# Adding the causal mask of the first attention on VectorE instead of TensorE

## The chip, the core and the metric

The program runs on one core of a Trainium2 chip. Five engines work side by side, each through its own queue in strict order: PE (TensorE, matmuls; its weight loads are listed as PEld), DVE (VectorE), ACT (ScalarE), POOL (GpSimd) and SP (SyncE, which issues DMAs here). They wait for each other through semaphores. The metric is the device time of one execution in microseconds (us); lower is better.

## The reference

Two transformer layers over 2 sequences of 1024 tokens and 256 channels. Only the first attention is touched by the change:

```python
q = einsum('bsd,hed->bhse', x, W_Q)          # 16 heads of width 128, k and v alike
scores = einsum('bhse,bhme->bhsm', q, k) / sqrt(128)
scores = where(causal, -1e9, scores)         # causal: key index > query index
pattern = softmax(scores)
z = einsum('bhsm,bhme->bhse', pattern, v)
out = einsum('bhse,hde->bsd', z, W_O)
```

After it come a layer norm, a mixture of 8 experts with a shared one, a second attention with grouped keys, and a mixture of 16 experts.

## The kernel before

Every matmul of fp32 data is done three times, with operands split into a high part (rounded to fp32r by ACT) and a low part (the difference, taken by DVE or POOL): `mm3` (L80 to L88) issues high x high at L86, and two cross terms at L87 and L88.

The first attention is `causal_attention`. It takes 32 "heads", numbered `hb` (16 heads of two sequences), one after the other. A head has 8 units, `qt` 0 to 7, one for each tile of 128 queries; tile `qt` has `(qt + 1) * 128` keys, so the keys beyond the diagonal block are never computed and only the diagonal 128x128 block needs a mask. A unit's scores lie in PSUM in one of two buffers, `s_ps[:, qt % 2]`.

What one tile goes through, with the engine of each step:

- PE `scores`: the three matmuls for every 512 keys, then one matmul of identity and mask that adds the mask to the diagonal block (L876) and reports `s_ready`.
- DVE `maximum` (L1054): negated row maximum `negm`, reports `max_done`.
- ACT `soften` (L972): exp of the scores with their sum, into `pr`, reports `exp_done`.
- DVE `invert` (L1063): reciprocal of the sum. POOL `normalise` (L830): `pr` times that, reports `p_done`.
- PE `turn` (L886): transposes of `pr` into `t_ps`, in one batch of up to 4 blocks or in two.
- ACT `keep_hi` (L979) writes `pth`; DVE `keep_lo` (L1070) writes `ptl` and frees the `t_ps` buffer (`tl_done`), of which there are two.

The steps of several tiles run at once. In unit `qt`, the order written out by hand is:

- PE: `scores(qt + 2)`, `turn(qt)`, then the unit's tasks
- ACT: `keep_hi(qt)`, `soften(qt + 2)`, then the tasks' high parts
- DVE: `invert(qt + 1)`, `maximum(qt + 2)`, `keep_lo(qt)`, then the tasks' low parts

Here `qt + 2` beyond 7 means a tile of the next head. Below, a prime marks such a tile: in unit 6 DVE takes the maximum of tile 0'. The tasks are the projections of the next head (`q`, `k`: high part at L1003, low part at L1088 and L1091), the product with the values (`pv`, for queries 512 to 1023 of the last head in unit 0, and for 0 to 511 in unit 4; it gives `zh`, `zl`), and the output projection `o` (added into `yT` by DVE, L1082). Each fourth head (`hb % 4 == 0`, called a lead head here) has one more task in each unit, the values of four heads (`v`). The other 24 are called plain heads. Three of these (17 to 19) carry the norm and the router of the first sequence too. All tasks share two PSUM banks, so a task on PE waits until DVE has emptied that of the last but one.

Of the kernel before, what the change touches and what calls it, by code (L numbers as in the profile page):

```python
# [8 lines left out]
F32R = mybir.dt.float32r  # L9
ACT = mybir.ActivationFunctionType  # L10
ALU = mybir.AluOpType
AX = mybir.AxisListType

P = 128
# [68 lines left out]
def mm3(pe, out, a_hi, a_lo, b_hi, b_lo, first, last):  # L83


    pe.matmul(out, a_hi, b_hi, start=first, stop=False)  # L86
    pe.matmul(out, a_hi, b_lo, start=False, stop=False)  # L87
    return pe.matmul(out, a_lo, b_hi, start=False, stop=last)  # L88
# [524 lines left out]
def causal_attention(nc, tag, counters, a, xh, xl, yT, ident, idr, eps, psum, rw, norm, router):  # L613
# [5 lines left out]
    NQ = S // P  # L619
# [5 lines left out]
    MASKED = -1.0e30  # L625
# [44 lines left out]
    with Phase(nc, tag, psum) as ph:  # L670
# [10 lines left out]
        qh = ph.sb("qh", [P, 2, S], F32R)  # L681
        ql = ph.sb("ql", [P, 2, S], F32R)
        kh = ph.sb("kh", [P, 2, S], F32R)
        kl = ph.sb("kl", [P, 2, S], F32R)
# [7 lines left out]
        negm = ph.sb("negm", [P, NP])  # L692
        rsum = ph.sb("rsum", [P, NP])
        rinv = ph.sb("rinv", [P, NP])
        mask0 = ph.sb("mask0", [P, P])
        mask = ph.sb("mask", [P, P], F32R)
        s_ps = ph.ps([P, 2, S])
        t_ps = ph.ps([P, 2, CH])
        r_ps = ph.ps([P, 2, CH])
# [1 line left out]
        cleared = ph.sem("cleared")  # L701
# [3 lines left out]
        mask_set = ph.sem("mask_set")  # L705
        rounded = ph.sem("rounded")
# [8 lines left out]
        wol_done = ph.sem("wol_done")  # L715
        s_ready = ph.sem("s_ready")
        max_done = ph.sem("max_done")
        exp_done = ph.sem("exp_done")
        inv_done = ph.sem("inv_done")
        p_done = ph.sem("p_done")  # L720
# [42 lines left out]
        def after(hb, qt):  # L763

            u = hb * NQ + qt
            return u // NQ, u % NQ

        @block.sync
        def _(sp):
            def load_x(c):  # L770
                t = slice(c * CH, (c + 1) * CH)
                sp.dma_start(yT[:, :, t], a["xT"][:, :, t]).then_inc(y_in[c], 16)

            def load(n):
                if n >= 2:

                    sp.wait_ge(wl_done, (n - 1) * 2)
                sp.dma_start(wr[:, n % 2], a["qkv0"][n % H0, :, 0:2]).then_inc(wr_in[n % 2], 16)

            def load_v(g):  # L780
                if g >= 1:
                    sp.wait_ge(wvl_done, g)
                h0 = g * VG % H0
                for h in range(VG):
                    sp.dma_start(wvr[:, :, h, :], a["qkv0"][h0 + h, :, 2]).then_inc(wv_in, 16)

            def load_o(n):
                if n >= 1:
                    sp.wait_ge(wol_done, n)
                sp.dma_start(wor[:], a["o0"][n % H0]).then_inc(wor_in, 16)  # L790

            load(0)
            load_x(0)
            load_x(1)
            load_v(0)
            load(1)
            load_o(0)
            load_x(2)
            load_x(3)
            rw.sync(sp)  # L800
            for hb in range(HB):
                if hb + 2 < HB:
                    load(hb + 2)
                if hb + 1 < HB:
                    load_o(hb + 1)
                if hb % VG == 0 and hb + VG < HB:
                    load_v(hb // VG + 1)

        @block.gpsimd
        def _(pool):  # L810
            def split(n):
                pool.wait_ge(wh_done, n + 1)
                for w in range(2):
                    pool.tensor_tensor(wl[:, n % 2, w].rearrange("p t e -> p (t e)"), wr[:, n % 2, w].rearrange("p t e -> p (t e)"),
                                       wh[:, n % 2, w].rearrange("p t e -> p (t e)").bitcast(F32),
                                       ALU.subtract).then_inc(wl_done, 1)

            def split_v(g):
                pool.wait_ge(wvh_done, g + 1)
                pool.tensor_tensor(wvl[:].rearrange("p t e -> p (t e)"), wvr[:].rearrange("p t h e -> p (t h e)"),  # L820
                                   wvh[:].rearrange("p t e -> p (t e)").bitcast(F32), ALU.subtract).then_inc(wvl_done, 1)

            def split_o(n):
                pool.wait_ge(woh_done, n + 1)
                pool.tensor_tensor(wol[:], wor[:], woh[:].bitcast(F32), ALU.subtract).then_inc(wol_done, 1)

            def normalise(hb, qt):
                pool.wait_ge(inv_done, hb * NQ + qt + 1)
                j, n = qt % NP, (qt + 1) * P
                pool.tensor_tensor(pr[j][:, 0:n], pr[j][:, 0:n], rinv[:, j:j + 1].to_broadcast([P, n]),  # L830
                                   ALU.mult).then_inc(p_done, 1)

            pool.memset(ident[:], 0.0).then_inc(cleared, 1)
            pool.memset(mask0[:], 0.0).then_inc(cleared, 1)
            pool.memset(eps[:], EPS).then_inc(eps_set, 1)
            pool.wait_ge(cleared, 1)
            pool.affine_select(out=ident[:], in_=ident[:], compare_op=ALU.not_equal, fill=1.0, base=0,
                               pattern=[[-1, P]], channel_multiplier=1).then_inc(ident_done, 1)
            pool.wait_ge(cleared, 2)

            pool.affine_select(out=mask0[:], in_=mask0[:], compare_op=ALU.is_ge, fill=MASKED, base=0,
                               pattern=[[-1, P]], channel_multiplier=1).then_inc(mask_set, 1)
            split(0)
            split_v(0)
            normalise(0, 0)
            split(1)
            split_o(0)
            for hb in range(HB):
                for qt in range(NQ):
                    if after(hb, qt + 1)[0] < HB:  # L850
                        normalise(*after(hb, qt + 1))
                    if qt == 2 and hb + 2 < HB:
                        split(hb + 2)
                    if qt == 4 and hb >= 1:
                        split_o(hb)
                    if qt == 5 and hb % VG == 2 and hb + 2 < HB:
                        split_v(hb // VG + 1)

        @block.tensor
        def _(pe):  # L860
            def scores(hb, qt):
                u = hb * NQ + qt
                if qt == 0:
                    pe.wait_ge(task_out, PLACE[hb - 1, ("k", 0)] + 1)
                if qt == CQ:
                    pe.wait_ge(task_out, PLACE[hb - 1, ("k", 1)] + 1)
                if u >= 2:

                    pe.wait_ge(exp_done, u - 1)
                q0, s = qt * P, hb % 2  # L870
                keys = q0 + P
                for k0 in range(0, keys, CH):
                    k1 = min(keys, k0 + CH)
                    mm3(pe, s_ps[:, qt % 2, k0:k1], qh[:, s, q0:q0 + P], ql[:, s, q0:q0 + P], kh[:, s, k0:k1], kl[:, s, k0:k1],
                        True, k1 < keys)
                pe.matmul(s_ps[:, qt % 2, q0:q0 + P], idr[:], mask[:], start=False, stop=True).then_inc(s_ready, 1)  # L876

            def turn(hb, qt):
                pe.wait_ge(p_done, hb * NQ + qt + 1)
# [59 lines left out]
            pe.wait_ge(ident_done, 1)  # L939
            for t in PRE:  # L940
                task((-1, t))
            pe.wait_ge(rounded, 2)
            for qt in range(2):
                scores(0, qt)
            for hb in range(HB):
                for qt, tasks in enumerate(PLANS[hb]):
                    if qt < NQ:
                        if after(hb, qt + 2)[0] < HB:
                            scores(*after(hb, qt + 2))
                        turn(hb, qt)  # L950
                    for t in tasks:
                        if t[0] == "side":
                            t[1].tensor(pe, t[2], ring)
                        else:
                            task((hb, t))

        @block.scalar
        def _(act):
# [51 lines left out]
                task((-1, t))  # L1010
            act.wait_ge(mask_set, 1)
            act.wait_ge(eps_set, 1)
            act.activation(mask[:], mask0[:], ACT.Copy).then_inc(rounded, 1)
            act.activation(idr[:], ident[:], ACT.Copy).then_inc(rounded, 1)
            for t in PRE[2:]:
                task((-1, t))
# [28 lines left out]
        def _(dve):  # L1045
# [5 lines left out]
            def maximum(hb, qt):  # L1051
                dve.wait_ge(s_ready, hb * NQ + qt + 1)
                n = (qt + 1) * P
                dve.tensor_reduce(negm[:, qt % NP:qt % NP + 1], s_ps[:, qt % 2, 0:n], AX.X, ALU.max,  # L1054
                                  negate=True).then_inc(max_done, 1)

# [40 lines left out]
            for qt in range(2):  # L1097
                maximum(0, qt)
# [656 lines left out]
def program(nc, a, out):  # L1755
    with ExitStack() as stack:
# [51 lines left out]
        with Phase(nc, "g") as g:  # L1808
            rw0 = RouterWeights(g, "rw0", w0, True)
            n0a = norm(g, "n0a", 0)  # L1810
            r0a = router(g, "r0a", 0, rw0, "n0a")
            causal_attention(nc, "a0", counters, a, xh, xl, yT, ident, idr, eps, psum, rw0, n0a, r0a)

            z = [g.sb(f"z{b}", [P, S // P, D]) for b in range(B)]
# [136 lines left out]
```

## Time and profile before

| | us |
|---|---|
| median of 3 runs | 2251.52 |
| lowest and highest of them | 2243.45, 2257.3 |
| the profiled execution, device time | 2240.75 |
| its span, first to last instruction | 2238.6 |
| mean granted TensorE clock | 0.977 |

Of the 2238.6 us, the first attention takes about the first 990; its heads are periodic, four by four. The profiled execution is 10.8 us (0.5%) below the median of the three runs. 2.15 us of its time lie outside the span. Matmul durations in the trace run from issue to the last result, so they overlap: what a matmul costs PE is read from the distance between the starts of neighbours, not from its own duration.

### The profile page before, as it was taken

How to read it: one execution, taken by the hardware profiler on the slowest of the kernel's cores; microseconds unless marked ns; L12 is line 12 of the kernel's file. 1: busy time of each engine (PE TensorE's matmuls, PEld its weight loads, DVE VectorE, ACT ScalarE, POOL GpSimd, SP SyncE). 2: the span in 40 equal slices, each digit the busy share in tenths (PEclk: the TensorE clock that was granted, in tenths of full speed). 3: DMA queues.
4: the chain of work that ended last, by engine and by line, in shares of the span. 5: the costliest groups of instructions: out<-in, count | busy, mean ns of one | idle time of the engine just before them, and what ended most of it. 6: DMA issues, size and time to landing. Idle time of an engine off the chain costs nothing. (4 is left out here: it accounts for less than half of the span.)

```text
span 2238.6 us, 30499 instructions
## 1 busy us (share of the span) xinstructions
PE 2125.4 (95%) x11008; PEld 1608.0 (72%) x11008; DVE 1455.6 (65%) x2505; ACT 1207.5 (54%) x2425; POOL 556.9 (25%) x543
## 2 busy tenths in 40 slices
PE   7999999999999999989999968999998699999998
PEld 5888888888888888867788853333333487787886
DVE  4666666666766666656656547888883656645554
ACT  5655556565656565534444442877777334434344
POOL 3433434343424343322222210000000012221221
PEclk9999999999999999999999995999999799999999
DMA  2000000000000000011111120100000011111111
GB/s 80 15 9 24 15 24 15 24 15 24 8 24 15 24 15 15 6 31 46 43 43 43 43 42 16 23 16 22 16 22 1 27 36 43 43 50 43 48 45 61
DMA packets 54297, 64.74 MB, mean 29 GB/s; under 512 B 9179, under 2 KB 34566, under 8 KB 54150
## 3 DMA queue, kind: packets, MB, share of 16 engines
q1 hardware_dynamic: 54150, 62.81, 10.1%
q8 instruction: 89, 1.46, 0.3%
q14 instruction: 58, 0.48, 0.1%
HBM read 52.68 MB, written 2.10 MB: 24 GB/s over the span
## 5 line engine op out<-in xcount | busy, mean ns | idle before, releaser
L830 POOL TENSOR_TENSOR a_pr<-a_pr,a_rinv 128x128 f32<-128x128 f32 (+7 forms) x256 | 294.2, 1149 | 514.9 <-DVE a_rinv L1063 514.7
L1675 DVE TENSOR_REDUCE a_negm<-psum 128x1 f32<-128x1024 f32 x256 | 301.4, 1219 | 49.2 <-PE psum L1553 48.4
L1227 POOL TENSOR_TENSOR f_lo_gu<-f_raw_gu,f_hi_gu 128x512 fp32r<-128x512 f32 x84 | 108.9, 1296 | 848.4 <-ACT f_hi_gu L1313 848.4
L1656 ACT ACTIVATE a_pt<-psum 128x512 f32<-128x512 f32 x512 | 268.2, 602 | 81.8 <-PE psum L1568 81.5
L86 PE MATMUL psum<-xh,f_hi_gu 128*128 128x512 f32 x672 | 269.4, 401 | 7.0 <-DVE f_hid L1385 6.8
L1396 DVE TENSOR_TENSOR f_hl<-f_hid,f_hh 128x512 fp32r<-128x512 f32 x168 | 116.6, 694 | 236.6 <-ACT f_hh L1338 234.8
L88 PE MATMUL psum<-xh,f_lo_gu 128*128 128x512 f32 x672 | 263.8, 393 | 0.0
L87 PE MATMUL psum<-xl,f_hi_gu 128*128 128x512 f32 x672 | 263.5, 392 | 0.0
L1327 ACT ACTIVATE f_act_s<-psum,f_bias 128x512 f32<-128x512 f32 x168 | 115.1, 685 | 270.6 <-PE psum L88 270.4
L979 ACT ACTIVATE a_pth<-psum 128x512 fp32r<-128x512 f32 (+3 forms) x384 | 174.7, 490 | 142.9 <-PE psum L886 140.5
L972 ACT ACTIVATE a_pr<-psum,a_negm 128x128 f32<-128x128 f32 (+7 forms) x256 | 190.4, 744 | 81.8 <-DVE a_negm L1054 76.9
L1553 PE MATMUL psum<-x_ks,a_qq 48*128 48x512 f32 x512 | 186.3, 475 | 19.3 <-DMA a_qq<-x_qlo 14.5
L1070 DVE TENSOR_TENSOR a_ptl<-psum,a_pth 128x512 fp32r<-128x512 f32 (+3 forms) x384 | 200.3, 549 | 6.1 <-ACT a_pth L979 5.7
L1054 DVE TENSOR_REDUCE a_negm<-psum 128x1 f32<-128x128 f32 (+7 forms) x256 | 189.5, 741 | 2.9 <-PE psum L876 0.7
L1338 ACT ACTIVATE f_hh<-f_hid 128x512 fp32r<-128x512 f32 x168 | 105.5, 628 | 158.9 <-DVE f_hid L1390 151.8
L886 PE MATMUL psum<-ident,a_pr 128*128 128x128 f32 x1152 | 171.8, 276 | 10.7 <-POOL a_pr L830 9.0
L1568 PE MATMUL psum<-a_qq,x_ks 49*128 49x512 f32 x512 | 171.2, 480 | 4.5 <-ACT a_pt L1656 4.1
L1568 PEld LDWEIGHTS psum<-a_qq,x_ks 49*128 49x128 f32 x512 | 67.8, 187 | 138.5 <-ACT a_pt L1656 136.6
L86 PEld LDWEIGHTS psum<-xh,f_hi_gu 128*128 128x128 f32 x672 | 127.3, 189 | 40.2 <-DVE f_hid L1385 10.2
L1385 DVE SCALAR_TENSOR_TENSOR f_hid<-psum,f_bias,f_act_s 128x512 f32<-128x512 f32 x168 | 125.2, 745 | 43.8 <-PE psum L88 33.5
L1091 DVE TENSOR_TENSOR a_zl<-psum,a_zh 128x512 fp32r<-128x512 f32 x64 | 44.2, 691 | 161.5 <-ACT a_zh L1003 161.5
L1553 PEld LDWEIGHTS psum<-x_ks,a_qq 48*128 48x128 f32 x512 | 95.8, 200 | 74.4 <-DVE a_negm L1675 44.5
(299 smaller groups left out, 4823.4 us busy)
## 6 DMA issues: line engine op xcount, KB each, us to landing
f_raw_gu<-in_gu SPq DMA_DIRECT2D x84, 256.0 KB, 2.7
f_raw_dn<-in_down SPq DMA_DIRECT2D x84, 128.0 KB, 2.0
a_wr<-in_qkv SPq DMA_DIRECT2D x32, 256.0 KB, 2.8
a_wvr<-in_qkv SPq DMA_DIRECT2D x32, 128.0 KB, 2.5
a_wor<-in_o SPq DMA_DIRECT2D x32, 128.0 KB, 2.0
a_qq<-x_qhi SPq DMA_DIRECT2D x128, 32.0 KB, 2.0
yT<-in_xT SPq DMA_DIRECT2D x4, 512.0 KB, 6.2
a_qq<-x_qlo SPq DMA_DIRECT2D x64, 32.0 KB, 2.0
```

Of the source, the lines that this page charges most:

```text
L86: pe.matmul(out, a_hi, b_hi, start=first, stop=False)
L87: pe.matmul(out, a_hi, b_lo, start=False, stop=False)
L88: return pe.matmul(out, a_lo, b_hi, start=False, stop=last)
L830: pool.tensor_tensor(pr[j][:, 0:n], pr[j][:, 0:n], rinv[:, j:j + 1].to_broadcast([P, n]), ALU.mult).then_inc(p_done, 1)
L972: act.activation(pr[qt % NP][:, 0:n], s_ps[:, qt % 2, 0:n], ACT.Exp, bias=negm[:, qt % NP:qt % NP + 1], accum_out=rsum[:, qt % NP:qt % NP ...
L979: act.activation(pth[c][:, rows_of(c, k0, count, qt % CQ), :], t_ps[:, n % 2, 0:count * P].rearrange("p (k q) -> p k q", q=P), ACT.Copy).t ...
L1054: dve.tensor_reduce(negm[:, qt % NP:qt % NP + 1], s_ps[:, qt % 2, 0:n], AX.X, ALU.max, negate=True).then_inc(max_done, 1)
L1070: dve.tensor_tensor(ptl[c][:, p, :], t_ps[:, n % 2, 0:count * P].rearrange("p (k q) -> p k q", q=P), pth[c][:, p, :].bitcast(F32), ALU.sub ...
L1553: m = pe.matmul(mx_ps[:, bank, half, :], qq[p0:p0 + ROWS, u % QSLOT, g % 2, q * P:(q + 1) * P], ks[b][p0:p0 + ROWS, g % 2, half * CH:(half ...
L1568: pe.matmul(st_ps[:, n % 3, :], ks[b][p0:p0 + ROWS + 1, g % 2, kt * P:(kt + 1) * P], qq[p0:p0 + ROWS + 1, u % QSLOT, g % 2, :], start=True ...
L1656: act.activation(pt[:, s % SLOTS, g, :], st_ps[:, n % 3, :], ACT.Exp, scale=1.0 / HD1).then_inc(exp_done, 1)
L1675: dve.tensor_reduce(negm[:, u % 2, g * NQ + q:g * NQ + q + 1], mx_ps[:, bank, :, :], AX.XY, ALU.max, negate=True).then_inc(mx_taken, 1)
```

## The change

PE no longer adds the mask. The last of the three score matmuls closes the sum and reports `s_ready`. DVE, at the head of `maximum`, adds the mask, now an fp32 tile that POOL makes once, to the diagonal block in place in PSUM, waits for that add to be finished (`masked`) and then takes the maximum. ACT no longer rounds the mask once to fp32r.

```diff
             pool.memset(ident[:], 0.0).then_inc(cleared, 1)
-            pool.memset(mask0[:], 0.0).then_inc(cleared, 1)
+            pool.memset(mask[:], 0.0).then_inc(cleared, 1)
...
                 for k0 in range(0, keys, CH):
                     k1 = min(keys, k0 + CH)
-                    mm3(pe, s_ps[:, qt % 2, k0:k1], qh[:, s, q0:q0 + P], ql[:, s, q0:q0 + P], kh[:, s, k0:k1], kl[:, s, k0:k1],
-                        True, k1 < keys)
-                pe.matmul(s_ps[:, qt % 2, q0:q0 + P], idr[:], mask[:], start=False, stop=True).then_inc(s_ready, 1)
+                    i = mm3(pe, s_ps[:, qt % 2, k0:k1], qh[:, s, q0:q0 + P], ql[:, s, q0:q0 + P], kh[:, s, k0:k1],
+                            kl[:, s, k0:k1], True, True)
+                i.then_inc(s_ready, 1)
...
-            pe.wait_ge(rounded, 2)
+            pe.wait_ge(rounded, 1)
...
-            act.activation(mask[:], mask0[:], ACT.Copy).then_inc(rounded, 1)
             act.activation(idr[:], ident[:], ACT.Copy).then_inc(rounded, 1)
...
             def maximum(hb, qt):
                 dve.wait_ge(s_ready, hb * NQ + qt + 1)
                 n = (qt + 1) * P
+                own = s_ps[:, qt % 2, n - P:n]
+                if (hb, qt) == (0, 0):
+                    dve.wait_ge(mask_set, 1)
+                dve.tensor_tensor(own, own, mask[:], ALU.add).then_inc(masked, 1)
+                dve.wait_ge(masked, hb * NQ + qt + 1)
                 dve.tensor_reduce(negm[:, qt % NP:qt % NP + 1], s_ps[:, qt % 2, 0:n], AX.X, ALU.max,
                                   negate=True).then_inc(max_done, 1)
```

On DVE, units 1 to 3 of head 1, a plain head. Before (a_zl belongs to the end of unit 0; a_ql is the low part of the `q` task of unit 1):

```order
54 L1091 TENSOR_TENSOR a_zl<-psum,a_zh 128x512 [waits side_rounded]
55 L1063 RECIPROCAL a_rinv<-a_rsum 128x1 [waits a0_p_done,a0_exp_done]
56 L1054 TENSOR_REDUCE a_negm<-psum 128x1 [waits a0_s_ready]
57 L1070 TENSOR_TENSOR a_ptl<-psum,a_pth 128x2x128 [waits a0_th_done]
58 L1088 SCALAR_TENSOR_TENSOR a_ql<-psum,a_qh 128x512 [waits side_rounded]
59 L1063 RECIPROCAL a_rinv<-a_rsum 128x1 [waits a0_p_done,a0_exp_done]
60 L1054 TENSOR_REDUCE a_negm<-psum 128x1 [waits a0_s_ready]
```

and in the changed kernel:

```order
66 L1095 TENSOR_TENSOR a_zl<-psum,a_zh 128x512 [waits side_rounded]
67 L1067 RECIPROCAL a_rinv<-a_rsum 128x1 [waits a0_p_done,a0_exp_done]
68 L1056 TENSOR_TENSOR psum<-psum,a_mask 128x128 [waits a0_s_ready]
69 L1058 TENSOR_REDUCE a_negm<-psum 128x1 [waits a0_masked]
70 L1074 TENSOR_TENSOR a_ptl<-psum,a_pth 128x2x128 [waits a0_th_done]
71 L1092 SCALAR_TENSOR_TENSOR a_ql<-psum,a_qh 128x512 [waits side_rounded]
72 L1067 RECIPROCAL a_rinv<-a_rsum 128x1 [waits a0_p_done,a0_exp_done]
73 L1056 TENSOR_TENSOR psum<-psum,a_mask 128x128 [waits a0_s_ready]
74 L1058 TENSOR_REDUCE a_negm<-psum 128x1 [waits a0_masked]
```

One add stands ahead of every maximum, in all 256 units; the maximum waits for it, and all else keeps its order.

On PE, the border of units 0 and 1 of the same head: the scores of tile 3, the transposes of tile 1, and the `q` task. Before:

```order
356 L86 MATMUL psum<-a_kh,a_qh 128x512 [waits a0_exp_done]
357 L87 MATMUL psum<-a_kl,a_qh 128x512
358 L88 MATMUL psum<-a_kh,a_ql 128x512
359 L876 MATMUL psum<-a_mask,idr 128x128
360 L886 MATMUL psum<-ident,a_pr 128x128 [waits a0_tl_done,a0_p_done]
361 L886 MATMUL psum<-ident,a_pr 128x128
362 L86 MATMUL psum<-xh,a_wh 128x512 [waits a0_wl_done,side_emptied]
```

and in the changed kernel:

```order
337 L86 MATMUL psum<-a_kh,a_qh 128x512 [waits a0_exp_done]
338 L87 MATMUL psum<-a_kl,a_qh 128x512
339 L88 MATMUL psum<-a_kh,a_ql 128x512
340 L886 MATMUL psum<-ident,a_pr 128x128 [waits a0_tl_done,a0_p_done]
341 L886 MATMUL psum<-ident,a_pr 128x128
342 L86 MATMUL psum<-xh,a_wh 128x512 [waits a0_wl_done,side_emptied]
```

The matmul of L876 is gone, and the transposes follow the scores at once; PE's waits are the same.

## Rows read from the trace of the kernel before

**Rows 1.** The page, part 1: busy time, share of span, instructions.

```profile
PE 2125.4 (95%) x11008; PEld 1608.0 (72%) x11008; DVE 1455.6 (65%) x2505; ACT 1207.5 (54%) x2425; POOL 556.9 (25%) x543
```

**Rows 2.** One window inside the first attention: busy us by engine, clock.

```profile
784.00:896.00 112.00, 110.56 (x625) 96.10 (x625) 74.20 (x152) 66.81 (x146) 46.66 (x44) 1.00 0.05 15
```

**Rows 3.** Groups by line, 60 to 1150 us: busy, mean ns, idle before and releaser.

```profile
L972 ACT ACTIVATE a_pr<-psum,a_negm 128x384 f32<-128x384 f32 (+1 forms) x246 | 183.6, 746 | 76.3 <-DVE a_negm L1054 71.4
L1054 DVE TENSOR_REDUCE a_negm<-psum 128x1 f32<-128x384 f32 (+1 forms) x246 | 183.0, 744 | 2.7 <-PE psum L876 0.4
L876 PE MATMUL psum<-a_mask,idr 128*128 128x128 f32 x246 | 58.2, 236 | 0.0
```

**Rows 4.** Timeline (start, us, engine), PE at the mask matmul, units 5 and 6.

```profile
435.06 0.39 PE L88 MATMUL psum<-a_kh,a_ql 128*128 128x512 f32 x1
...
435.29 0.22 PE L876 MATMUL psum<-a_mask,idr 128*128 128x128 f32 x1
...
435.35 0.82 PE L886 MATMUL psum<-ident,a_pr 128*128 128x128 f32 x6
...
437.68 0.27 PE L876 MATMUL psum<-a_mask,idr 128*128 128x128 f32 x1
437.79 0.95 PE L886 MATMUL psum<-ident,a_pr 128*128 128x128 f32 x7
```

**Rows 5.** Groups by line and shape on DVE, 60 to 970 us.

```profile
L1070 DVE TENSOR_TENSOR a_ptl<-psum,a_pth 128x256 fp32r<-128x256 f32 x61 | 25.2, 413 | 0.0
L1070 DVE TENSOR_TENSOR a_ptl<-psum,a_pth 128x128 fp32r<-128x128 f32 x62 | 17.4, 280 | 0.0
```

**Rows 6.** Timeline of DVE: an operation that waits for the one before it.

```profile
2228.94 0.41 DVE L226 BATCH_NORM_STATS2 g_n3b_stats<-psum 128x6 f32<-128x256 f32 x1
2229.39 0.25 DVE L229 BATCH_NORM_AGGREGATE g_n3b_mv<-g_n3b_stats 128x2 f32<-128x6 f32 x2
```

**Rows 7.** Timeline, head 13, units 1 to 3: DVE and ACT in turn.

```profile
422.83 0.69 DVE L1091 TENSOR_TENSOR a_zl<-psum,a_zh 128x512 fp32r<-128x512 f32 x1 [4.95 <-ACT a_zh L1003]
...
423.51 0.67 DVE L1054 TENSOR_REDUCE a_negm<-psum 128x1 f32<-128x512 f32 x1
...
424.21 0.69 ACT L972 ACTIVATE a_pr<-psum,a_negm 128x512 f32<-128x512 f32 x1 [0.60 <-DVE a_negm L1054]
...
425.51 0.69 DVE L1088 SCALAR_TENSOR_TENSOR a_ql<-psum,a_qh 128x512 fp32r<-128x512 f32 x1 [1.00 <-ACT a_qh L1003]
...
426.12 0.15 DVE L1063 RECIPROCAL a_rinv<-a_rsum 128x1 f32<-128x1 f32 x1
```

**Rows 8.** Timeline, head 13, units 3 to 6: where ACT or DVE wait for PE.

```profile
430.39 0.60 ACT L1003 ACTIVATE a_kh<-psum 128x512 fp32r<-128x512 f32 x1 [0.38 <-PE psum L88]
...
434.07 0.60 ACT L1003 ACTIVATE a_zh<-psum 128x512 fp32r<-128x512 f32 x1 [0.17 <-PE psum L88]
...
435.31 0.15 DVE L1063 RECIPROCAL a_rinv<-a_rsum 128x1 f32<-128x1 f32 x1
...
435.55 1.23 DVE L1054 TENSOR_REDUCE a_negm<-psum 128x1 f32<-128x1024 f32 x1
...
440.16 0.60 ACT L1003 ACTIVATE a_kh<-psum 128x512 fp32r<-128x512 f32 x1 [0.17 <-PE psum L88]
```

**Rows 9.** Timeline, head 13, unit 7 and the next head's first transpose.

```profile
439.38 1.90 POOL L830 TENSOR_TENSOR a_pr<-a_pr,a_rinv 128x1024 f32<-128x1024 f32 x1 [1.95 <-DVE a_rinv L1063]
...
441.33 1.09 PE L886 MATMUL psum<-ident,a_pr 128*128 128x128 f32 x8
...
442.65 1.29 DVE L1070 TENSOR_TENSOR a_ptl<-psum,a_pth 128x512 fp32r<-128x512 f32 x2
...
443.56 0.27 PE L886 MATMUL psum<-ident,a_pr 128*128 128x128 f32 x1
```

**Rows 10.** Timeline, head 14, unit 7: DVE's wait in such heads.

```profile
469.33 1.29 DVE L1070 TENSOR_TENSOR a_ptl<-psum,a_pth 128x512 fp32r<-128x512 f32 x2 [0.35 <-ACT a_pth L979]
```

**Rows 11.** Timeline, lead head 12, unit 6: DVE's wait there.

```profile
410.02 0.69 DVE L1091 TENSOR_TENSOR a_kl<-psum,a_kh 128x512 fp32r<-128x512 f32 x1 [0.57 <-ACT a_kh L1003]
```

More of the change, by code:

```diff
@@ L694, in causal_attention @@
         rinv = ph.sb("rinv", [P, NP])
-        mask0 = ph.sb("mask0", [P, P])
-        mask = ph.sb("mask", [P, P], F32R)
+        mask = ph.sb("mask", [P, P])
         s_ps = ph.ps([P, 2, S])
@@ L717, in causal_attention @@
         max_done = ph.sem("max_done")
+        masked = ph.sem("masked")
         exp_done = ph.sem("exp_done")
@@ L839, in _ @@
             pool.wait_ge(cleared, 2)
-            pool.affine_select(out=mask0[:], in_=mask0[:], compare_op=ALU.is_ge, fill=MASKED, base=0,
+            pool.affine_select(out=mask[:], in_=mask[:], compare_op=ALU.is_ge, fill=MASKED, base=0,
                                pattern=[[-1, P]], channel_multiplier=1).then_inc(mask_set, 1)
```

## The prediction

> **What bounds the kernel now.** Start with the page's part 1: PE is busy 95% of the span, DVE 65% [rows 1]. In a window inside the first attention PE is busy 110.56 of 112 us at a granted clock of 1.00, DVE 74.20, ACT 66.81, POOL 46.66 [rows 2]. Read alone, that says that anything taken from PE is gained and that DVE has room for more. Two further views correct it. The groups by line show who waits for whom: ACT's exp sat idle 71.4 us for DVE's maximum, while DVE's maximum hardly ever waited for PE (0.4 us) [rows 3]. So DVE is not ahead of the scores but behind them, and ACT hangs on DVE. The timeline of one plain head then shows that DVE and ACT hand work to each other with hardly a gap: the maximum of tile 3 ends at 424.18, exp starts at 424.21; the high part of `q` follows that exp on ACT, its low part starts on DVE at 425.51, and the next reciprocal follows [rows 7]. PE is full, but a chain over DVE and ACT is nearly as long as PE's own, and it is reset only in unit 0, where the long `pv` leaves DVE idle 4.95 us [rows 7]. At the end of a plain head the chain already holds PE up: the transposes of tile 7 start at 441.33, when POOL's 1.90 us from 439.38 are over at 441.28 [rows 9].
>
> **What is removed.** 256 mask matmuls. Their mean duration is 236 ns [rows 3], but durations overlap. At the end of a 512-column score matmul the starts are 435.06, 435.29 and 435.35: the mask holds PE for 0.06 us [rows 4]. Where the last score matmul has 128 columns, the mask starts at 437.68 and the transposes at 437.79: 0.11 us [rows 4]. Tiles 0 and 4 of a head are of the second kind, the other six of the first (also with 256 or 384 columns in the last part), so a head saves 6 x 0.06 + 2 x 0.11 = 0.58 us where PE sets the pace, and all 32 at most 18.6 us. ACT's one rounding of the mask and the wait for it are gone too, once, for nothing that I can count.
>
> The Trainium skill, "TensorE: Matmul & The Clock Gate", section "Back-to-back issue gap", gives about 81 ns for each 128-column load and matmul in a stream; by that the 256 would be worth 20.7 us, an estimate. The trace's 0.06 and 0.11 lie on either side of it.
>
> **What is added.** 256 adds of 128x128 on DVE, PSUM and SBUF in, PSUM out, and a wait of DVE for its own result. No DVE row of this trace writes PSUM. The nearest is the low part of 128x128, PSUM and SBUF in, SBUF out: 280 ns [rows 5]. An operation that waits for its predecessor starts after its end: 2229.35 to 2229.39, 0.04 us [rows 6]. One that does not wait starts some 0.08 us before that end: `a_ql` ends at 426.20 (425.51 + 0.69), the reciprocal starts at 426.12 [rows 7]. So one add delays its maximum by p = 0.28 + 0.04 = 0.32 us. The low end for p is 0.20 (280 ns less the overlap of 0.08, a wait that costs nothing); the high end is 0.45, that of an operation twice as wide, 413 ns [rows 5], and 0.04. I take 0.32, since the 280 ns row differs only in where it writes. The one wait for `mask_set` in tile 0 of head 0 is over long before.
>
> Behind the waiting maximum on DVE are queued the low parts of the transposes and of the tasks; behind the late maximum on ACT are exp, then the high part of a task, for which DVE waits again. So one late maximum delays both engines. With 8 adds a head this is 2.6 us of work in a chain that has less slack than that. Follow it through head 13.
>
> **The walk, plain head.** The chain starts fresh after `pv` of unit 0. Seven maxima lie on it until DVE has freed the transpose buffer that PE needs for the first transpose of the next head (tiles 3, 4, 5, 6, 7, 0', 1'): 7 p. Slack on the way takes something back. Before `a_kh` of unit 3, ACT waits 0.38 us for PE; before `a_zh` of unit 4, 0.17; the maximum of tile 7 starts at 435.55 although the reciprocal ahead of it lets it go at 435.38, since the scores came late, 0.17; before `a_kh` of unit 6 ACT waits 0.17 [rows 8]. Last, of the low parts in unit 7 (442.65 on, 1.29 us for two, so the first ends near 443.34) PE's transpose at 443.56 needs the first, and needs it 0.05 earlier (POOL's end at 441.28 to PE's start at 441.33 shows this latency): 0.17 [rows 9]. The slack is 0.38 + 4 x 0.17 = 1.06 us. A plain head gets 7 x 0.32 - 1.06 = 1.18 us longer. PE's saving is then worth nothing in it: PE arrives earlier and waits longer, in the transposes of tiles 3, 6 and 7 and of tile 0'.
>
> In the plain heads with `hb % 4 == 2` POOL has the next weights of `v` to split before it normalises tile 7, and DVE waits 0.35 us for ACT in unit 7 [rows 10]; that much more is absorbed: 0.83 us. Six regular heads are of this kind (after head 26 no weights are left to prepare).
>
> **Lead head.** The `v` task gives PE work in each unit that DVE and ACT need less for. In unit 6 DVE waits 0.57 us before `a_kl` [rows 11], more than the 0.32 that the add puts ahead of it. Here PE's saving is real, 0.58 us.
>
> **The sum.** Regular plain heads: 15 x 1.18 = 17.7. Those with POOL's split: 6 x 0.83 = 5.0. The three that host norm and router have more on PE, and I give them half, 3 x 0.6 = 1.8. Lead heads: 8 x -0.58 = -4.6. Together +19.9 us; on the profiled execution's 2240.75 that is 2260.7, or +0.89%. The runs shown have a median 0.5% above that execution; applied to the median, 2251.5 x 1.0089 = 2271.5. A measurement of this kernel can tell about 1%, 22.5 us, from no change. The sum depends on p by 7 x 21 + 10 = 157 us for each us (seven adds in 21 heads, and half of that in the three hosts): p = 0.20 gives +1.1, p = 0.45 gives +40.3.
>
> **Rivals.**
> First, PE alone counts: all delay on DVE and ACT fits in slack that I don't see. Then 32 x 0.58 = 18.6 us are gained, 2233. For it: PE's 95%. Against: the walk, and the transposes of tile 7 that wait for POOL already.
> Second, the wait on DVE costs nothing, p between 0.20 and 0.28: +1.1 to +13.6, 2253 at the low end. Against: the gap of 0.04 after an end against an overlap of 0.08 [rows 6, 7]. The Trainium skill states this rule in "VectorE: DVE Perf Modes", section "The DRAIN you can't avoid": 8 copies with a semaphore after each took as long as 8 with one after the last. By that rule 2253 would come out; the trace does not agree with it, since operations without a wait overlap there.
> Third, slower: the add in place costs more than the row of 280 ns, because it writes its 128 columns to PSUM, where it also reads, and the maximum must find them there. Its place is the same chain, its price 157 us for each us, and it decides from p = 0.337 on, where the sum passes 22.5 us. At p = 0.45 it is 2251.5 + 40.5 = 2292. For it: only 0.017 us separate it from my value, and no row prices the write. Against: nothing in rows 5 hints at it.
> That the change does not do what it says is excluded: 256 matmuls are gone from PE and as many adds stand on DVE.
>
> **How the numbers follow.** My forecast (p from 0.28 to 0.337, walk as above) gets 0.43, the first rival 0.07, the second 0.12, the third 0.38. Only the first rival at its best reaches 1% faster: 0.02. Slower by over 1% is the third: 0.38. The rest, 0.60, is within 1%. The range runs from 2240, between the first rival and the low p, to the third rival's 2292.
>
> **What would show each step.** L876 gone from PE; DVE busy up by 256 x 0.28 = 72 us. Add rows of about 280 ns, the maximum some 0.32 us after the add's start. ACT's idle before exp for DVE up from 71.4 us. PE's waits for POOL's `a_pr` and DVE's `a_ptl` up; a plain head's period up by about 1.2 us, a lead head's down by 0.6. I am wrong if the add is not near 0.28 us, if ACT or DVE keep more slack than the five places hold, or if the clock, 1.00 in the window [rows 2], falls because PE waits more.

## The result, and the profile after

| | before | changed |
|---|---|---|
| median of 4 runs, us | 2250.76 | 2276.92 |
| lowest, highest | 2243.45, 2257.3 | 2267.94, 2277.83 |
| profiled execution, span | 2240.75, 2238.6 | 2277.32, 2275.2 |

The changed kernel takes 1.0108 times as long, 95% interval 1.0068 to 1.0148: 24 us more (the two medians in the table lie 26 us apart). The forecast was 20 us more. The value lies slightly above the 1% that the prediction took as the least that can be told from no change, but the interval reaches to both sides of 1%, so which side of it the true value lies on isn't settled.

The page of the changed kernel, part 1, answers to [rows 1]:

```profile
PE 2137.4 (94%) x10752; PEld 1586.4 (70%) x10752; DVE 1524.2 (67%) x2761; ACT 1199.4 (53%) x2424; POOL 556.7 (24%) x543
```

256 instructions fewer on PE, 256 more on DVE, whose busy time is up by 68.6 us. The groups by line, from 60 to 1150 us as in [rows 3], with the new add:

```profile
L1058 DVE TENSOR_REDUCE a_negm<-psum 128x1 f32<-128x384 f32 (+1 forms) x246 | 187.2, 761 | 8.5
L972 ACT ACTIVATE a_pr<-psum,a_negm 128x384 f32<-128x384 f32 (+1 forms) x246 | 183.3, 745 | 182.3 <-DVE a_negm L1058 182.3
...
L1056 DVE TENSOR_TENSOR psum<-psum,a_mask 128x128 f32<-128x128 f32 x246 | 69.0, 280 | 0.0
```

The add takes 280 ns, exactly what the row of the same shape that writes to SBUF took [rows 5]. ACT's idle time before exp rose from 71.4 to 182.3 us. What waits for that is seen in the waits of PEld from 60 to 1000 us (total, times, longest). Before:

```profile
PEld psum L886 <- POOL a_pr L830: 13.2, 25, 1.9
PEld psum L86 <- DVE yT L1082: 2.5, 7, 0.4
```

Changed:

```profile
PEld psum L886 <- POOL a_pr L830: 39.2, 69, 2.5
...
PEld psum L86 <- DVE yT L1086: 5.9, 9, 0.7
```

PE waits for POOL's `a_pr` in 69 transposes instead of 25. The same can be followed in the timeline of the changed kernel, head 13, units 1 to 3, against [rows 7]:

```profile
430.71 0.69 DVE L1095 TENSOR_TENSOR a_zl<-psum,a_zh 128x512 fp32r<-128x512 f32 x1 [4.61 <-ACT a_zh L1003]
...
431.39 0.28 DVE L1056 TENSOR_TENSOR psum<-psum,a_mask 128x128 f32<-128x128 f32 x1
...
431.70 0.69 DVE L1058 TENSOR_REDUCE a_negm<-psum 128x1 f32<-128x512 f32 x1
...
432.43 0.69 ACT L972 ACTIVATE a_pr<-psum,a_negm 128x512 f32<-128x512 f32 x1 [1.00 <-DVE a_negm L1058]
...
434.33 0.15 DVE L1067 RECIPROCAL a_rinv<-a_rsum 128x1 f32<-128x1 f32 x1
434.40 0.28 DVE L1056 TENSOR_TENSOR psum<-psum,a_mask 128x128 f32<-128x128 f32 x1
...
434.72 0.82 DVE L1058 TENSOR_REDUCE a_negm<-psum 128x1 f32<-128x640 f32 x1
...
435.66 0.66 PE L886 MATMUL psum<-ident,a_pr 128*128 128x128 f32 x4 [0.21 <-POOL a_pr L830]
```

Each maximum starts 0.31 to 0.32 us after its add, and the delay travels: the reciprocal after `a_ql` comes 3.62 us after `a_zl` began (434.33 - 430.71), before it was 3.29 (426.12 - 422.83, [rows 7]); the transposes of tile 3, which had not waited, now wait for POOL. At the head's end, against [rows 9]:

```profile
449.92 1.09 PE L886 MATMUL psum<-ident,a_pr 128*128 128x128 f32 x8 [0.41 <-POOL a_pr L830]
...
451.55 1.28 DVE L1074 TENSOR_TENSOR a_ptl<-psum,a_pth 128x512 fp32r<-128x512 f32 x2
...
452.38 0.30 PE L886 MATMUL psum<-ident,a_pr 128*128 128x128 f32 x1
```

The start of the first transpose of each head (the row of 452.38 is that of head 14) gives the length of a head. Before, heads 12, 13, 14 and 15 start at 378.00, 416.22, 443.56 and 470.22; in the changed kernel at 386.02, 424.04, 452.38 and 479.71. The lead head 12 went from 38.22 to 38.02 us, the plain head 13 from 27.34 to 28.34, head 14 (POOL's split) from 26.66 to 27.33. The three hosts together, from the start of head 17 to that of 20, went from 91.23 (534.75 to 625.98) to 96.48 (545.00 to 641.48), and head 0 from 38.67 to 39.38. With these as samples of their kinds, 15 x 1.00 + 6 x 0.67 + 5.25 - 7 x 0.20 + 0.71 = 23.6 us. The last transpose of the first attention starts at 976.3 before and at 1000.1 after, 23.8 us later.

The two profiled executions differ by 36.6 us, 12.8 more than that. These 12.8 us lie behind the first attention, in code that the change doesn't touch. Windows counted from the last transpose show where, in the clock column (the last but two). Before:

```profile
976.00:1300.00 324.00, 313.90 (x1400) 252.61 (x1398) 195.57 (x323) 138.28 (x246) 71.91 (x70) 0.98 0.17 46
1300.00:1400.00 100.00, 73.21 (x270) 39.60 (x268) 65.00 (x85) 34.54 (x63) 3.59 (x4) 0.71 0.11 23
1700.00:1800.00 100.00, 77.68 (x375) 44.31 (x375) 38.44 (x101) 45.62 (x83) 5.32 (x5) 0.88 0.07 20
```

Changed:

```profile
1000.00:1324.00 324.00, 313.84 (x1399) 252.43 (x1398) 195.81 (x323) 138.58 (x247) 71.83 (x70) 0.98 0.16 46
1324.00:1424.00 100.00, 73.70 (x250) 39.14 (x248) 62.41 (x82) 31.70 (x57) 3.59 (x4) 0.66 0.12 23
1724.00:1824.00 100.00, 78.53 (x339) 39.27 (x336) 33.54 (x95) 45.25 (x83) 3.29 (x3) 0.76 0.05 15
```

The granted clock is a mean over its two levels, 1.2 and 2.4 GHz. The second window of each three lies at the start of the second attention, the third at its end; PE is busy 73 to 79 of 100 us there in either kernel. In both, the clock was lower in this execution (0.66 for 0.71, 0.76 for 0.88). That this belongs to the execution and not to the change is shown below.

### The profile page after: what moved, and what is told of

It is laid out like the page before. It is cut to its first block and busy times, and to the rows that moved or that the text cites. A ratio compares the mean times of both kernels' runs of the same rounds, so it can differ in the third digit from the quotient of the medians.

```text
span 2275.2 us, 30243 instructions
## 1 busy us (share of the span) xinstructions
PE 2137.4 (94%) x10752; PEld 1586.4 (70%) x10752; DVE 1524.2 (67%) x2761; ACT 1199.4 (53%) x2424; POOL 556.7 (24%) x543
## 5 line engine op out<-in xcount | busy, mean ns | idle before, releaser
L1572 PE MATMUL psum<-a_qq,x_ks 49*128 49x512 f32 x512 | 176.2, 494 | 4.2 <-ACT a_pt L1660 3.7
L886 PEld LDWEIGHTS psum<-ident,a_pr 128*128 128x128 f32 x1152 | 132.7, 141 | 58.7 <-POOL a_pr L830 40.7
```

The lines of the kernel that those rows point to most:

```text
L886: i = pe.transpose(t_ps[:, n % 2, k * P:(k + 1) * P], pr[qt % NP][:, (k0 + k) * P:(k0 + k + 1) * P], ident[:])
L1572: pe.matmul(st_ps[:, n % 3, :], ks[b][p0:p0 + ROWS + 1, g % 2, kt * P:(kt + 1) * P], qq[p0:p0 + ROWS + 1, u % QSLOT, g % 2, :], start=True ...
```

## The experiments

The table has the length of heads 12 (lead), 13 (plain) and 14 (plain, with POOL's split), from the starts of their first transposes, the start of the attention's last transpose, the span behind it, and the time against the kernel before with its interval. Each ratio is against runs of the kernel before made together with those of that kernel. Two columns need care. The span behind the last transpose differs by up to 18 us between traces of the same code, as shown at the end. The last transpose also holds the start-up and head 0, whose length follows the granted clock there: head 1 begins at 58.6 in the second trace of before (clock 0.96 in head 0), at 60.6 in the first (0.92) and at 62.9 in e9_lead_not5 (0.85). So differences of up to 4 us in that column are judged from the heads instead.

| kernel | 12 | 13 | 14 | last transpose | behind it | ratio |
|---|---|---|---|---|---|---|
| before | 38.22 | 27.34 | 26.66 | 976.3 | 1262.3 | 1 |
| changed | 38.02 | 28.34 | 27.33 | 1000.1 | 1275.1 | 1.0108 (1.0068 to 1.0148) |
| e1_no_mask | 37.65 | 27.04 | 26.42 | 965.9 | 1265.8 | 0.9933 (0.9911 to 0.9955) |
| e2_add_only | 38.59 | 28.27 | 27.32 | 1003.9 | 1264.1 | 1.0118 (1.0075 to 1.0162) |
| e3_add_early | 38.02 | 28.41 | 27.37 | 1001.4 | 1264.7 | 1.0111 (1.0069 to 1.0153) |
| e4_lead_only | 38.04 | 27.32 | 26.68 | 973.8 | 1277.4 | 1.0018 (0.9995 to 1.0041) |
| e5_placed | 37.65 | 27.11 | 26.59 | 973.1 | 1275.2 | 0.9991 (0.9970 to 1.0012) |
| e8_late_tiles | 38.24 | 27.85 | 26.90 | 987.0 | 1277.4 | 1.0068 (1.0038 to 1.0099) |
| e9_lead_not5 | 37.71 | 27.34 | 26.66 | 974.8 | 1268.0 | one run |
| e7_two_adds | 39.18 | 30.82 | 29.63 | 1066.0 | 1264.9 | 1.0423 (1.0390 to 1.0455) |
| e10_placed_hosts | 37.69 | 27.16 | 26.54 | 968.4 | 1280.1 | 0.9965 (0.9943 to 0.9986) |
| e11_before_again | 38.19 | 27.31 | 26.66 | 974.2 | 1262.1 | one run |

The theory on trial is that of the walk: in plain heads a chain over DVE and ACT sets the length, the adds lengthen it by 0.32 us each less some slack, and PE's saving counts in lead heads only. Its rival: PE sets the pace everywhere, and the loss comes from elsewhere.

**Half the change: no mask at all.**

```diff
-                dve.tensor_tensor(own, own, mask[:], ALU.add).then_inc(masked, 1)
-                dve.wait_ge(masked, hb * NQ + qt + 1)
```

> The changed kernel without the add: no mask is applied anywhere in the first attention, neither on PE nor on VectorE, so its time shows what taking the matmul away is worth alone. Chain theory (VectorE and ScalarE set a plain head's length from the scores of tile 7 to the transposes of tile 7, PE the rest): lead heads 0.58 us shorter, plain heads about 0.4, the end of the first attention some 14 us earlier than in the kernel before. PE theory (every matmul taken from PE is gained): 0.58 us in every head, 18.6 us earlier. If the matmuls were hidden: no change.

The kernel leaves the mask out altogether. The last transpose came 10.4 us earlier, not 14. The lead head gained 0.57 us, to the 0.01 what the distances of starts had given. The plain ones gained 0.30 and 0.24, less than the 0.4 expected. In head 13 the transposes of tile 7 still wait for POOL, whose product of that tile ends 24.82 us after the head's first transpose (434.67 + 1.89 - 411.74) where it was 25.06 (441.28 - 416.22): so only 0.24 us of what PE saved ahead of them comes through, to which the mask of tile 2', behind them, adds 0.06. The masks of tiles 0' and 1', which stand between the scores of tile 7 and those transposes, count for nothing. Why POOL isn't earlier still was not followed. The PE theory's 18.6 us are ruled out. With the other engines' order as it is, these 10.4 us are the most that moving the mask elsewhere could have brought.

**The other half: the add alone.** PE keeps its matmul, DVE adds a tile of zeros.

```diff
+                dve.tensor_tensor(own, own, zero[:], ALU.add).then_inc(masked, 1)
+                dve.wait_ge(masked, hb * NQ + qt + 1)
                 dve.tensor_reduce(negm[:, qt % NP:qt % NP + 1], s_ps[:, qt % 2, 0:n], AX.X, ALU.max,
```

> The kernel before, with PE's mask matmul, plus an add of a tile of zeros on VectorE ahead of each maximum, with its wait. Chain theory: plain heads 1.0 to 1.2 us longer than before, those with POOL's split 0.7 to 0.9, lead heads 0 to 0.3; the first attention ends 23 to 30 us later. If the loss came from somewhere else (the score sum that is closed earlier, PE's order), this kernel would be within 5 us of the one before.

27.6 us later, and plain heads are as long as with the whole change (28.27 and 28.34, 27.32 and 27.33). So all that the change costs is the add, and in a plain head taking the matmul away as well returns nothing. In the lead head it returns 0.57 us (38.59 to 38.02). But the add cost the lead head 0.37 us, for which my walk had nothing.

**Where the lead head loses.** The waits of PEld had it: PE waits for `yT` in seven lead heads, 0.4 us each before, 0.7 with the add. In unit 3 the `v` task needs the bank that the addition into `yT` empties; on DVE that addition stands behind the maximum of tile 5. First the adds in lead heads alone:

```diff
+        def on_vector(hb, qt):
+            return (hb * NQ + qt) >= 2 and ((hb * NQ + qt - 2) // NQ) % VG == 0
...
+                if not on_vector(hb, qt):
+                    i = pe.matmul(s_ps[:, qt % 2, q0:q0 + P], idr[:], mask[:], start=False, stop=True)
```

> VectorE adds the mask only for the tiles whose maximum falls in the units of lead heads; all others keep PE's matmul. Chain theory: plain heads as before, lead heads as with the change, 0.2 to 0.3 us shorter than before or up to 0.58; first attention 2 to 5 us earlier, within 0.3% of before in total. If VectorE's work slows all heads alike, lead heads are 1 us longer.

0.18 us gained in head 12, below the 0.2 to 0.58 expected, plain heads unchanged. The last transpose came 2.5 us earlier, 1.6 of it from head 1 on. In its trace, the waits of PEld:

```profile
PEld psum L86 <- DVE yT L1096: 5.2, 7, 0.7
```

Then the same without tile 5:

> As the run with adds in lead heads only, but tile 5 is masked by PE there. If the wait of PE for yT in unit 3 of a lead head is what took back part of its gain: lead heads 0.5 us shorter than before instead of 0.16 to 0.19. If the adds of all tiles slow it: 0.2 us.

Head 12 took 37.71 us, 0.51 less than before, and the wait is back where it was:

```profile
PEld psum L86 <- DVE yT L1096: 2.5, 7, 0.4
```

One add of eight, at the one place where PE waits for what stands behind it, took back more than half of the lead head's gain; the 0.51 that is left is the 0.57 of e1 less the 0.06 of the one matmul that PE keeps.

**A shorter wait.** VectorE adds first, takes the reciprocal in the meantime, then the maximum.

```diff
                         if after(hb, qt + 2)[0] < HB:
+                            add_mask(*after(hb, qt + 2))
+                        if after(hb, qt + 1)[0] < HB:
                             invert(*after(hb, qt + 1))
                         if after(hb, qt + 2)[0] < HB:
                             maximum(*after(hb, qt + 2))
```

> The changed kernel with one step moved: VectorE adds the mask ahead of the reciprocal, and the reciprocal fills the time until the add is finished, so that the maximum hardly waits. By the rows of before the maximum then comes about 0.25 us late instead of 0.32. Chain theory: 7 x 0.07 = 0.5 us less in a plain head than with the change, the first attention ends 9 to 12 us earlier than in the changed kernel. If the wait costs nothing, as with the change, or a later reciprocal takes back what is gained: no difference.

A miss: no gain. The timeline of DVE in this kernel shows why:

```profile
435.03 0.69 DVE L1103 SCALAR_TENSOR_TENSOR a_ql<-psum,a_qh 128x512 fp32r<-128x512 f32 x1 [1.00 <-ACT a_qh L1008]
435.64 0.29 DVE L1070 TENSOR_TENSOR psum<-psum,a_mask 128x128 f32<-128x128 f32 x1
435.84 0.15 DVE L1078 RECIPROCAL a_rinv<-a_rsum 128x1 f32<-128x1 f32 x1
436.03 0.82 DVE L1060 TENSOR_REDUCE a_negm<-psum 128x1 f32<-128x640 f32 x1
```

The reciprocal does overlap the add's end (it starts 0.20 us after it), but the maximum, which waits for `masked`, starts 0.04 us after the reciprocal's end at 435.99 instead of 0.08 before it. From the end of `a_ql`'s turn to the maximum it is 0.39 us (435.64 to 436.03), as in the changed kernel (434.33 to 434.72), and the reciprocal, for which POOL waits, is later. So it is in 250 of the 254 places of this order in the trace. One of the other four shows that it isn't the wait as such:

```profile
986.82 0.29 DVE L1070 TENSOR_TENSOR psum<-psum,a_mask 128x128 f32<-128x128 f32 x1
987.42 0.16 DVE L1078 RECIPROCAL a_rinv<-a_rsum 128x1 f32<-128x1 f32 x1 [0.31 <-ACT a_pr L977]
987.50 0.82 DVE L1060 TENSOR_REDUCE a_negm<-psum 128x1 f32<-128x640 f32 x1
```

Here the reciprocal itself was held up, the add had been over for 0.31 us when it began, and the maximum starts 0.08 us before the reciprocal's end at 987.58, wait or no wait. At 435.93 the add had ended only 0.06 us before the reciprocal's end: too late for that.

**Dose: two adds for one.**

```diff
                 dve.tensor_tensor(own, own, mask[:], ALU.add).then_inc(masked, 1)
-                dve.wait_ge(masked, hb * NQ + qt + 1)
+                dve.wait_ge(masked, (hb * NQ + qt) * 2 + 1)
+                dve.tensor_tensor(own, own, zero[:], ALU.add).then_inc(masked, 1)
+                dve.wait_ge(masked, (hb * NQ + qt) * 2 + 2)
```

> The changed kernel with a second add, of a tile of zeros, after the first, with its own wait. Chain theory: no slack is left after the first, so seven times 0.32 us more in a plain head, which gets 2.2 us longer than with the change (30.5 to 30.6 us); the last transposes 50 to 60 us later than in the changed kernel. If slack absorbed most of it again: some 23 us later, as for the first.

65.9 us later than the changed kernel; heads 13 and 14 got 2.48 and 2.30 us longer. The first add cost 1.00 and 0.67. So slack of more than a microsecond had taken its share of the first, and nothing is left for the second: 7 x 0.32 is 2.24 (the 0.24 above that in head 13 wasn't followed). The lead head too, at 39.18, is 1.16 us longer than with the first add alone. The total is above the expected range by 6 us.

**Place: three adds for each plain head, early or late on the chain.** Early (tiles 2, 4, 5; in lead heads all but 5):

```diff
+        def on_vector(hb, qt):
+            return hb * NQ + qt >= 2 and (qt != 5 if ((hb * NQ + qt - 2) // NQ) % VG == 0 else qt in (2, 4, 5))
```

> VectorE adds the mask only where the walk says that its chain has slack (tiles 2, 4 and 5 of plain heads) or PE sets the pace (in the units of lead heads, all but tile 5, whose late maximum holds back the addition into yT for which PE waits in unit 3); PE keeps the rest. Chain theory: plain heads 0.2 us shorter than before, lead heads 0.5 us, the last transposes of the first attention 6 to 9 us earlier than in the kernel before, 0.3 to 0.4% in total. If an add costs a plain head its 0.32 us wherever it stands: plain heads 0.7 us longer.

Late (tiles 7, 0' and 1' in the units of plain heads, none in those of lead heads):

```diff
+        def on_vector(hb, qt):
+            return hb * NQ + qt >= 2 and ((hb * NQ + qt - 2) // NQ) % VG != 0 and qt in (7, 0, 1)
```

> Also three adds for each plain head, but for tiles 7, 0' and 1', late on the chain; lead heads as before. Chain theory: 3 x 0.32 less slack of 0.17 at three places, plain heads 0.4 to 0.5 us longer than before, the last transposes 9 to 12 us later. If only the number of adds counts, the same as with tiles 2, 4 and 5.

Early, plain heads 13 and 14 are 0.23 and 0.07 us shorter than before, late 0.51 and 0.24 longer: the same number of adds, opposite signs. The late kernel's last transpose is 10.7 us later, within the 9 to 12 expected, but with help from head 0, which took 37.90 us there at a clock of 0.95: from the start of head 1 it is 928.2 us, 12.5 more than the 915.7 of before, and 2.2 of these are the hosts' (93.40 for 91.23). The early one's came 3.2 us earlier, not 6 to 9. Two things are in the way. Head 0 took 41.16 us (21.51 to 62.67) instead of 38.67. The granted clock in it was 0.84 in this trace and 0.92 in that of before; in the second trace of before, and in the next kernel, whose adds in head 0 are the same as here, head 0 took 37.76 at 0.96, so that part is the clock's. From the start of head 1 to the last transpose it is 910.4 us instead of 915.7, 5.3 less. And the heads that host norm and router, head 17 to head 20, took 92.38 us (533.15 to 625.53), 1.15 more than before, at a clock of 1.00 in both: that part is not the clock's.

**A version that gains.** Heads 17 to 19 keep PE's matmul:

```diff
-            return hb * NQ + qt >= 2 and (qt != 5 if ((hb * NQ + qt - 2) // NQ) % VG == 0 else qt in (2, 4, 5))
+            return hb * NQ + qt >= 2 and (qt != 5 if ((hb * NQ + qt - 2) // NQ) % VG == 0
+                                          else qt in (2, 4, 5) and not H0 < hb < H0 + VG)
```

> As the run with adds placed where there is slack, but heads 17 to 19, which also carry the norm and the router, keep PE's mask matmul in all their tiles. Chain theory: these three return to their length of before (30.5, 30.5, 30.1 us), the last transposes come 5 to 6 us earlier than in the kernel before, 0.2% in total, at the edge of what can be measured. If the placed adds cost something elsewhere: no earlier than in that run.

The last transpose starts at 968.4, 7.9 us earlier than in the first trace of before and 5.8 than in the second. Head 17 to head 20 took 91.13 us (529.58 to 620.71), as before. The ratio is 0.9965 (0.9943 to 0.9986): faster than the kernel before by 0.35%, 8 us, and 1.4% faster than the changed one by the two ratios (the two were not run together). That is below what the prediction took as the least that can be told, though the interval leaves out 1; and part of it may be where the clock fell. The windows from head 1 to the last transpose, here and in the first trace of before, are the better evidence:

```profile
59.00:968.40 909.40, 886.31 (x4950) 761.35 (x4949) 645.89 (x1409) 533.61 (x1184) 361.40 (x343) 1.00 0.06 17
60.60:976.20 915.60, 893.54 (x5062) 773.68 (x5061) 615.55 (x1296) 538.35 (x1184) 361.82 (x343) 1.00 0.06 17
```

6.2 us less at a granted clock of 1.00 in both, and the second trace of before also has 915.6 (58.6 to 974.2). The rest of the 7.9 lies in the start-up and head 0, with their clocks of 0.96 and 0.92.

**The stages behind.**

> The kernel before, unchanged, for a second trace of it. The stages behind the first attention are the same code in all kernels here, yet took 1263 us in the trace of before and 1276 in that of the changed kernel. If this follows how long the granted clock is low there, and not the change, a second trace of the same kernel may show either value, with the low clock to match; the first attention should end at 976 us again, within 1 us.

The second trace of before has 974.2 for the last transpose (2.1 us from the first; 1 was expected) and 1262.1 behind it, the first value again. This run alone doesn't separate the two. The other kernels do: all run the same code there. The add-only kernel with all 256 adds took 1264.1 behind the last transpose, the one with adds in lead heads only 1277.4. Windows of these two, at the same distance from the last transpose as above, first with all adds:

```profile
1328.00:1428.00 100.00, 72.93 (x267) 39.44 (x265) 64.69 (x84) 33.69 (x62) 3.58 (x4) 0.69 0.12 23
1728.00:1828.00 100.00, 77.65 (x375) 43.54 (x368) 38.30 (x101) 46.05 (x84) 5.33 (x5) 0.88 0.07 20
```

then with adds in lead heads only:

```profile
1298.00:1398.00 100.00, 72.13 (x260) 38.74 (x258) 63.91 (x84) 33.17 (x60) 3.59 (x4) 0.69 0.12 24
1698.00:1798.00 100.00, 79.14 (x325) 38.52 (x324) 31.29 (x92) 42.64 (x78) 3.29 (x3) 0.71 0.04 12
```

So the low clock around the end of the second attention goes with the execution, not with the number of adds. The changed kernel shows it by itself: one of its four runs had a mean clock of 0.973 and took 2267.94 us, the other three 0.968 to 0.969 and 2276.52 to 2277.83. And the 19 runs of the kernel before made together with e1 to e4 range from 2241.50 us at a mean clock of 0.976 to 2257.82 at 0.966. What decides how an execution falls stays open.

## Why the prediction was right, point by point

- What is removed: the matmul's worth, read from starts, was right for a head in which PE sets the pace (0.58 forecast, 0.57 in e1 and between e2 and the changed kernel). The sum that let only lead heads profit was right too: with the add in place plain heads gained nothing from it.
- The add: 0.28 + 0.04 = 0.32 us forecast, 0.31 to 0.32 measured, 280 ns of it the add. The third rival, a dearer write to PSUM, fell: 280 ns is the price of the SBUF row. The time nonetheless came out just above 1%, by what lead heads, head 0 and hosts cost and not by the price.
- The second rival, a wait that costs nothing, fell: with the wait, the maximum starts 0.03 to 0.04 us after the add's end in all 256 units of the changed kernel, where the add, which needn't wait, starts some 0.08 before the reciprocal's end. e3 shows that a short operation in between doesn't bring the overlap back, unless the result waited for is long there.
- The first rival fell with e1 (10 us, not 18.6) and e2.
- The walk: 1.18 us forecast for a regular plain head, 1.00 measured; 0.83 and 0.67 with POOL's split. The slack is 0.18 us larger than I read. Places where ACT waited for PE hold more than their idle time, as ACT's rows ahead of `a_kh` in unit 3 show, before and in the changed kernel:

```profile
429.82 0.19 ACT L972 ACTIVATION_READ_ACCUMULATOR a_pr<-psum,a_negm 128x1 f32 x1
430.39 0.60 ACT L1003 ACTIVATE a_kh<-psum 128x512 fp32r<-128x512 f32 x1 [0.38 <-PE psum L88]
...
438.70 0.19 ACT L972 ACTIVATION_READ_ACCUMULATOR a_pr<-psum,a_negm 128x1 f32 x1
438.79 0.59 ACT L1003 ACTIVATE a_kh<-psum 128x512 fp32r<-128x512 f32 x1
```

Before, `a_kh` starts 0.38 us after the end of the operation ahead of it; once that is late, `a_kh` no longer waits for PE and starts 0.10 us before that end. So this place absorbs 0.48, and `a_zh` of unit 4 and `a_kh` of unit 6 likewise 0.27 each instead of 0.17. That makes 0.30 us more slack at three places, of which 0.18 show in the head; the remaining 0.12 are lost in small pieces that I haven't followed. That PE comes earlier in the changed kernel is not the reason: in e2 PE has its mask matmuls and head 13 is as little longer, 0.93 us. My sum has 3.7 us too much by this, over 21 heads.
- The lead head: this step of the prediction was wrong. "Here PE's saving is real, 0.58 us": measured 0.20. I looked at the wait for `a_kl` in unit 6, which has room, and not at that for `yT` in unit 3, which had none (e4 and e9). For seven heads that is 2.7 us too little, and head 0, 0.7 longer instead of 0.6 shorter, adds 1.3 (its start-up, with a clock of 0.92 in both traces, was not walked at all).
- The hosts: "more on PE, and I give them half" was wrong: +5.25 us instead of 1.8. They have more on DVE too, which was busy 66.70 of 91 us there before and 73.96 of 96 after, 73% and 77%, against 19.62 of 28 (70%) in head 14 before. Little of it is clock. Head by head the three take 32.53, 32.12 and 31.84 us in the changed kernel instead of 30.55, 30.54 and 30.14. In the windows of the first two (545.00:577.50 and 577.50:609.60) the granted clock is 1.00, so their 1.98 and 1.58 us are none of the clock's; only that of head 19, 1.70 longer, has 0.95 (609.60:641.40). In the add-only kernel the three took 95.93 us (547.36 to 643.29) at 0.99. Which wait makes the hosts dearer is open, but the three got their old length back when PE took their masks over again (e10).
- The sum: +19.9 forecast, +23.8 in the trace and 1.08% (24 us) in the runs. The walk's excess of 3.7 us is outweighed by the 7.4 that lead heads, head 0 and hosts cost more. The mechanism was right, the chain over DVE and ACT in plain heads and the price of the add; that the sum came within 4 us of the trace is partly luck, since these errors of opposite sign cancel in part. I gave within 1% a chance of 0.60 and slower by more 0.38; 1.08% is on the far side of that border by less than the width of its interval.

The Trainium skill's 81 ns for a 128-column matmul in a stream ("TensorE: Matmul & The Clock Gate", "Back-to-back issue gap") lies above the 71 ns that 0.57 us for the eight of a lead head makes.

## What to carry to other kernels

A full engine is not the bound of every stretch: before moving work from it to one that is 65% busy, follow one period of the loop from its last reset and ask what stands in queue behind the new work, on that engine and on the one that waits for it. Measure the idle times along that chain, since they are nearly all that a new operation may use, and look at every wait of the full engine, however short, for one that ends on what will be delayed. The same operation can gain at one place of the period and lose at another, so place it by position and not for all tiles alike.

## What I had not expected of the hardware

- On VectorE an operation with nothing to wait for starts 0.08 us before the end of the one ahead. One that waits for the result of the one ahead starts 0.04 us after its end. With a short third one between them it was 0.04 us after the end of that third one (435.99 to 436.03), so the short operation in the gap didn't help; only where the result had been there for 0.31 us did the overlap come back (987.50 against 987.58).
- On ScalarE the overlap with the operation ahead is 0.10 us (438.79 against 438.89), and it was missing where the later one had to wait for PE (430.39 against 430.01). There the idle time read from the trace was short of the slack by that much.
- An add of 128x128 in place in PSUM takes 280 ns, the same as with its output in SBUF.
- The stages behind the first attention, with the same code, took from 1262.1 to 1280.1 us in twelve traces. In the five for which the windows were read, the granted clock around the end of the second attention, where PE is busy under 80%, was 0.88 in the three with 1262 to 1264 us, 0.76 and 0.71 in the two with 1275 and 1277. This spread of 18 us is three quarters of what the whole change cost.
